# A vision tower on one core: the first pair of image groups worked through group by group, with images loaded first and products ahead of the data

## What is computed

```python
proj = patches(16x16) @ W.T + b                        # 36 patches of 768, EMBED 256
h    = concat([cls, proj]) + pos_embed                 # 37 tokens an image
q, k, v = split_heads(h @ Wq, h @ Wkv)                 # 16 heads of 64
sim  = q @ k.T / 8
G    = sigmoid(sim); P = min(reversed_cumsum(G), 63)
sim += interpolation of (q @ pos_emb) at P             # contextual positions
h    = layernorm(h + softmax(sim) @ v @ Wout + b_out)
# router over 8 experts, the best two of each token, and a shared expert
out  = layernorm(h + shared(h) + routed(h))
```

## Time and profile before

| what | us |
|---|---|
| runs | 784.12, 785.13, 785.18 (median 785.13) |
| the profiled execution | 790.15 |
| its span, first to last instruction | 788.4 |
| TensorE busy | 735.7 (93%) |
| DVE busy | 511.1 (65%) |
| ACT busy | 421.1 (53%) |
| POOL busy | 160.1 (20%) |
| mean granted TensorE clock | 0.971 |

### The profile page before, as it was taken

The page is one execution under the profiler, slowest core; times in us unless marked ns, Lnnn a source line. Parts: engine busy times, 40 slices in busy tenths (PEclk is TensorE's granted clock), DMA queues, the critical chain, the costliest instruction groups (busy, mean ns, idle before and its releaser), DMA issues. The chain is left out here.

```text
span 788.4 us, 14517 instructions
## 1 busy us (share of the span) xinstructions
PE 735.7 (93%) x5019; PEld 638.3 (81%) x5020; DVE 511.1 (65%) x1063; ACT 421.1 (53%) x780; POOL 160.1 (20%) x200
## 2 busy tenths in 40 slices
PE   5988999999999999999999979986999999999972
PEld 5867697979798897979797957775888999999862
DVE  0059898989798898989898988962442222222383
ACT  2365847565756758475656556321112555555264
POOL 2000000000000000000000000027532577776232
PEclk9999999999999999999999999988799999999997
DMA  8930001010102010010000033002001222221351
GB/s 294 315 117 17 19 24 45 23 45 23 45 0 65 3 41 27 23 34 23 12 23 12 6 119 113 23 15 25 1 2 31 66 78 83 87 83 55 141 172 71
DMA packets 28304, 47.36 MB, mean 60 GB/s; under 512 B 4794, under 2 KB 19108, under 8 KB 28275
## 3 DMA queue, kind: packets, MB, share of 16 engines
q1 hardware_dynamic: 22802, 37.24, 15.1%
q0 software_dynamic: 5472, 9.76, 4.0%
HBM read 35.57 MB, written 13.24 MB: 62 GB/s over the span
## 5 line engine op out<-in xcount | busy, mean ns | idle before, releaser
L584 POOL TENSOR_TENSOR rs<-ve,neg_half 111x2 f32<-111x2 f32 x11 | 12.5, 1133 | 472.6 <-DVE ve L1509 472.6
L758 PE MATMUL ps_X<-wkv_sb,hT 128*111 128x512 f32 (+1 forms) x176 | 85.7, 619 | 8.0 <-ACT v_sb L1150 7.5
L1034 PE MATMUL ps_S<-attnT,v_sb 128*128 128x128 f32 x704 | 85.9, 275 | 0.1
L1428 DVE COPY_PREDICATED table<-bit,table 111x112 f32<-111x112 int16 (+6 forms) x110 | 76.3, 694 | 11.4 <-DVE table L1428 0.2
L1034 PEld LDWEIGHTS ps_S<-attnT,v_sb 128*128 128x128 f32 x704 | 82.1, 192 | 0.3 <-issue 0.3
L1101 ACT COPY simS<-ps_S 32x666 f32<-32x666 f32 (+3 forms) x105 | 74.1, 705 | 13.4 <-DVE table L1485 10.5
L1758 DVE COPY attnT<-ps_S 128x256 f32<-128x256 f32 x44 | 18.7, 425 | 89.7 <-PE ps_S L1048 89.6
L758 PEld LDWEIGHTS ps_X<-wkv_sb,hT 128*111 128x111 f32 (+1 forms) x176 | 27.9, 174 | 50.7 <-issue 30.2
L699 PE MATMUL ps_S<-hT,wq_sb 128*128 128x222 f32 (+1 forms) x352 | 66.2, 345 | 0.0
L699 PEld LDWEIGHTS ps_S<-hT,wq_sb 128*128 128x128 f32 x352 | 63.5, 189 | 0.1
L794 PE MATMUL ps_X<-oT,wout_sb 128*128 128x222 f32 x320 | 61.9, 350 | 0.0
(11 more groups left out here) (212 smaller groups left out, 1383.5 us busy)
## 6 DMA issues: line engine op xcount, KB each, us to landing
down_sb<-in_x_dram SPq DMA_DIRECT2D x10, 648.0 KB
gu_sb<-y_d SPq DMA_DIRECT2D x8, 512.0 KB, 8.2
h_d<-hT SPq DMA_DIRECT2D x11, 222.0 KB, 2.7
kept<-h_d SPq DMA_DIRECT2D x11, 222.0 KB, 2.6
h_d<-h SPq DMA_DIRECT2D x10, 222.0 KB
wkv_sb<-in_L_attn_Wkv_dram SPq DMA_DIRECT2D x2, 1024.0 KB, 9.8
gu_sb<-in_L_ffn_gate_w_dram SPq DMA_DIRECT2D x2, 1024.0 KB, 11.2
gu_sb<-in_L_ffn_up_w_dram SPq DMA_DIRECT2D x2, 1024.0 KB, 12.3
```

The costliest lines, as they stand in the source:

```text
L758: mm = nc.tensor.matmul(X[:r, 1 - s], hT[:, k].rearrange("p b t -> p (b t)")[:, a * ROWS:a * ROWS + r], wkv_sb[:, k, INNER + 512 * s:INNER ...
L1034: mm = nc.tensor.matmul(S[:, i, j * FF + f * P:j * FF + f * P + P], held[:, i, k, j, f * P:f * P + P], xgT[:, i, k], start=(k == 0), stop= ...
L1428: A.did(V.copy_predicated(near[:, :, :, 0:SL - d], by_side(bit[:, n], r)[:, :, :, 0:SL - d], near[:, :, :, d:SL]))
```

## The change

- The images of pair 0 are loaded first. The token weights follow in three pieces of 256 columns, with a semaphore each. The six small loads are issued from ACT's queue.
- Half of pair 0's images is regrouped on POOL and half on DVE.
- TensorE starts with four products of the ones with the zeroed `gate` (`warm_up`), whose result is overwritten. Then it turns the patches of pair 0, and turns and multiplies the token weights piece by piece (`turn_tok`, `embed_part`). DVE, not ACT, copies the turned weights, and the two halves of an embedding (here and in pair 1) lie in two banks, and are added as each is done.
- Pair 0 has its own program, `first_pair`: keys and queries of group 0 alone (`by_group`, 111 columns), its score and values, then keys, part of the values, patches of pair 1, queries and the score of group 1. Then `embed(1)`, `keys(1)` and also `queries(1)`, before the weights of group 0 are turned. `pair(1)` is written out without its queries, and the loops of TensorE and ACT start at 2.
- DVE copies the first position table after ACT's copies of the scores, and adds `embed(1)` behind all seven parts of group 0's `cope`, not behind the fourth.

The diff, cut to its core:

```diff
+        def embedded(p, m):
+
+            if isinstance(p, int) and p < 2:
+                return X[:, m, :NPAT]
+            return X[:, 0, m * NPAT:(m + 1) * NPAT]
+
+        def of_group(bank):
+
+            return bank[:, :2 * ROWS].rearrange("p (f r) -> p f r", f=2)
+
+        KA_BANKS = [X[:, 0], S[:, 4], S[:, 5], X[:, 1]]
+        QA_BANKS = [S[:, 0], S[:, 3], S[:, 1], S[:, 2]]
+        KB_BANKS = [S[:, 0], S[:, 1], S[:, 2], S[:, 3]]
+        QB_BANKS = [S[:, 1], S[:, 2], S[:, 3], S[:, 4]]
...
+                    sp.wait_ge(xp_other, 1)
                 sp.dma_start(x_sb[:rows, :], x_rows[bass.ds(p * XR, rows), :]).then_inc(x_in, 16)
...
-            sp.dma_start(w_nat[:, :, :], tok_w.rearrange("(t p) d -> p t d", p=P)).then_inc(w_tok, 16)
             load_x(0, XR)
-            sp.dma_start(pe_nat[:TOK, :], pos_embed[0]).then_inc(w_small, 16)
...
-            for h in range(2):
-                sp.dma_start(cope_nat[DH * h:DH * h + DH, :], cope_emb).then_inc(w_small, 16)
+            for s in range(3):
+                cols = slice(2 * s * P, 2 * s * P + 2 * P)
+                sp.dma_start(w_nat[:, :, cols], tok_w.rearrange("(t p) d -> p t d", p=P)[:, :, cols]).then_inc(w_tok[s], 16)
...
-            regroup(0)
+            pool.wait_ge(x_in, 16)
+            nc.gpsimd.tensor_copy(xp_sb[:, :NPH // 2, :].rearrange("p r (i w) -> p r i w", w=PATCH),
+                                  x_halves[:, :NPH // 2]).then_inc(xp_ready, 1)
...
+                for j, bank in enumerate(second_banks if next_first(p) else patch_banks):
+                    if next_first(p) and j == 2:
+                        pe.wait_ge(k_sb, 1)
...
+            def by_group(bank, w, s, a):
+
+                for i in range(2):
+                    c = (2 * s + i) * P
+                    for k in range(KE):
+                        mm = nc.tensor.matmul(bank[:, i * ROWS:(i + 1) * ROWS], w[:, k, c:c + P],
+                                              hT[:, k, a * TPG:(a + 1) * TPG], start=(k == 0), stop=(k == KE - 1))
+                return mm
...
+                if first(p) and a == 0:
+                    pe.wait_ge(ka_sb, 4)
+                elif first(p):
+                    pe.wait_ge(k_sb, 4)
+                    pe.wait_ge(q_sb, 4)
+                    pe.wait_ge(xt_sb, 6)
+                elif a == 0:
                     pe.wait_ge(k_sb, p * 4 + 4)
                 for f in range(FT):
-                    if a == 0 and f % 3 == 0:
+                    if first(p):
+                        if a == 0 and f % 3 == 0:
+                            pe.wait_ge(qa_sb, 2 + f // 3)
+                    elif a == 0 and f % 3 == 0:
                         pe.wait_ge(q_sb, p * 4 + 2 + f // 3)
...
+            def first_pair():
+
+                pe.wait_ge(hT_ready, KE)
+                pe.wait_ge(w_k, 16)
+                for s in range(4):
+                    by_group(KA_BANKS[s], wkv_sb, s, 0).then_inc(ka_done, 1)
+                pe.wait_ge(w_q, 16)
+                for s in range(4):
+                    by_group(QA_BANKS[s], wq_sb, s, 0).then_inc(qa_done, 1)
+                pe.wait_ge(tables, N_TABLES)
+                score(0, 0)
+                for s in range(2):
+                    values(0, 0, s)
+                pe.wait_ge(sim_sb, 2)
+                pe.wait_ge(table_sb, 1)
+                for s in range(4):
+                    by_group(KB_BANKS[s], wkv_sb, s, 1).then_inc(k_done, 1)
+                values(0, 1, 0)
+                patches(1)
+                for s in range(4):
+                    if s < 3:
+                        pe.wait_ge(k_sb, s + 2)
+                    else:
+                        pe.wait_ge(xt_sb, 4)
+                    by_group(QB_BANKS[s], wq_sb, s, 1).then_inc(q_done, 1)
+                values(0, 1, 1)
+                score(0, 1)
+                pe.wait_ge(v_ready, 4)
+                pe.wait_ge(w_o, 16)
+                embed(1)
+                keys(1)
+                queries(1, True)
+                pe.wait_ge(q_sb, 4 + 2)
+                turn_weights(0, True)
+                pe.wait_ge(q_sb, 4 + 4)
+                outputs(0, 0)
+                patches(2)
+
             def pair(p, ahead, ahead2):
 
-                queries(p, ahead)
+                if next_first(p):
+                    pe.wait_ge(xt_sb, p * 3 + 6)
+                else:
+                    queries(p, ahead)
                 score(p, 0)
                 for s in range(2):
                     values(p, 0, s)
                 values(p, 1, 0)
-                if not first(p):
-                    turn_weights(p * 2 - 1, True)
+                turn_weights(p * 2 - 1, True)
                 values(p, 1, 1)
...
+            def warm_up(n):
+
+                for _ in range(n):
+                    nc.tensor.matmul(S[:, 2], ones[:, :], gate[:].rearrange("p h t -> p (h t)")[:, :512],
+                                     start=True, stop=True)
...
+            pe.wait_ge(consts, 5)
+            pe.wait_ge(zeroed, 1)
+            warm_up(4)
+            pe.wait_ge(consts, N_CONSTS)
+            pe.wait_ge(xp_other, 1)
+            patches(0)
+            turn_tok(0)
+            turn_tok(1)
+            pe.wait_ge(xt_sb, 3)
+            embed_part(0)
+            turn_tok(2)
+            embed_part(1)
...
-            pe.wait_ge(setup_sb, 1)
-            patches(0)
-            pe.wait_ge(setup_sb, 3)
-            embed(0)
-            pe.wait_ge(tables, N_TABLES)
-            pe.wait_ge(zeroed, 1)
-            keys(0)
-            patches(1)
-            pe.wait_ge(w_o, 16)
-            pair(0, True, True)
-            with pe.Fori(1, G2 - 2) as p:
+            embed_part(2)
+            first_pair()
+            pair(1, True, True)
+            with pe.Fori(2, G2 - 2) as p:
                 pair(p, True, True)
...
-                    if a == 0:
+                    if a == 0 and not first(p):
                         act.wait_ge(table_sb, g + 1)
...
+            def first_pair():
+
+                for s in range(4):
+                    act.wait_ge(ka_done, s + 1)
+                    nc.scalar.copy(kT[:, 2 * s:2 * s + 2, 0, :ROWS], of_group(KA_BANKS[s])).then_inc(ka_sb, 1)
+                for s in range(4):
+                    act.wait_ge(qa_done, s + 1)
+                    nc.scalar.copy(qT[:, 2 * s:2 * s + 2, :ROWS], of_group(QA_BANKS[s])).then_inc(qa_sb, 1)
+                for step in range(2):
+                    score(0, 0, step)
+                gates(0, 0)
+                for s in range(2):
+                    values(0, 0, s)
+                for s in range(4):
+                    act.wait_ge(k_done, s + 1)
+                    nc.scalar.copy(kT[:, 2 * s:2 * s + 2, 1, :ROWS], of_group(KB_BANKS[s])).then_inc(k_sb, 1)
+                distance(0)
+                values(0, 1, 0)
+                patches(1)
+                for s in range(4):
+                    act.wait_ge(q_done, s + 1)
+                    nc.scalar.copy(qT[:, 2 * s:2 * s + 2, ROWS:], of_group(QB_BANKS[s])).then_inc(q_sb, 1)
+                regroup(2)
+                values(0, 1, 1)
+                for step in range(2):
+                    score(0, 1, step)
+                tables_out(0, 1)
+                gates(0, 1)
+                softmax_exp(0)
+                for s in range(4):
+                    keys(1, s)
+                for s in range(4):
+                    queries(1, s)
+                weights(0)
+                distance(1)
+                outputs(0, 0)
+                patches(2)
+
             def pair(p, ahead, ahead2):
-                before = not first(p)
-                for s in range(2):
-                    queries(p, s)
+                if not next_first(p):
+                    for s in range(2):
...
-            act.wait_ge(setup_t, 3)
-            for s in range(3):
-                nc.scalar.copy(tokT[:, 2 * s:2 * s + 2], S[:, (2, 4, 5)[s]].rearrange("p (j e) -> p j e", j=2)
-                               ).then_inc(setup_sb, 1)
+            act.dma_start(pe_nat[:TOK, :], pos_embed[0]).then_inc(w_small, 16)
+            act.dma_start(pe_nat[TOK:TOK + 1, :], tok_b.rearrange("(a e) -> a e", a=1)).then_inc(w_small, 16)
...
+            for h in range(2):
+                act.dma_start(cope_nat[DH * h:DH * h + DH, :], cope_emb).then_inc(w_cope, 16)
...
-            for s in range(4):
-                keys(0, s)
-            patches(1)
             act.wait_ge(tables, N_TABLES)
-            pair(0, True, True)
-            with act.Fori(1, G2 - 2) as p:
+            first_pair()
+            pair(1, True, True)
+            with act.Fori(2, G2 - 2) as p:
...
             def embed(p):
-                dve.wait_ge(emb_done, p + 1)
                 if not first(p):
                     dve.wait_ge(h_saved, p * 16)
                 for m in range(KE):
-                    src = X[:, 0, m * NPAT:(m + 1) * NPAT].rearrange("p (c b r) -> p c b r", c=NPH, b=2 * TPG)
```

(18 more changed lines are left out.)

110 lines of the change are left out of this document (61 added, 49 removed).

## The result

| what | before | after |
|---|---|---|
| median of 5 runs each, side by side | 785.18 (784.12 to 787.36) | 779.70 (778.12 to 780.83) |
| ratio | | 0.992 (95%: 0.9899 to 0.9941) |
| profiled execution, its span | 790.15, 788.4 | 779.73, 778.0 |
| mean granted clock | 0.971 | 0.977 |
| first keys start | 22.74 | 17.26 |

The kernel is 5.5 us faster by the medians. The forecast was 776.4 (773.5 to 781.0): right in direction, inside the range, 3.3 us too low. The mark came at 77.56 against 77.1 forecast. Both kernels were run again in a second session: 785.35 (29 runs) against 776.75 (4 runs), ratio 0.9892 (0.9867 to 0.9918), which is 8.6 us. The two intervals overlap, so the runs alone don't show that the gains differ.

What follows compares the result with a forecast made beforehand. TensorE was taken to bound the kernel, busy 735.7 of 788.4 us. The 8.7 us gained early take the profiled execution from 790.15 to 781.5; less 5 us from profile to median gives 776.4 us (773.5 to 781.0).

Steps and rivals of the forecast that it cites:

- mark: Point where TensorE starts turning the second group's weights; forecast at 77.1 us, not 85.76.
- walk: TensorE's steps summed in order of time, from the start to the turning of the second group's weights: 8.7 us gained.
- given back at the loop: Rival: DVE's addition for the second pair waits for the first pair's hT save, 4 us lost, 780.4; chance 0.05.
- late save: Save of the first pair's hT, behind the expert weights in SP's queue; landing at 50 us would lose 4 us.
- 111-column product: Keys or queries of one group on TensorE: 3.2 us taken, half of the 222-column product; 3.6 by the 128-column form.
- two waits that were charged: TensorE idle before the second pair's score, for patches (1.5 us), and before the third product of values (1.5, previously 0.79).
- The parts: Gain by cause: 5.8 us head, 4.7 wait and half clock at 63 us, 1.0 shrinking waits, less 2.2: 9.3.
- last test: Whole forecast wrong if the second group's weights turn at 77 us and the end does not follow by 8.7.
- Low clock: Rival: TensorE's clock stays low through the setup, gain only 4.8 to 6.2 us, 779.6; chance 0.15.
- No new waits: Rival: ACT keeps up, so the added waits for patches and values don't arise; 10.9 us gained, 774.2; chance 0.12.
- No change: Rival: DVE or the queues, not TensorE, set the loop; 785 us; chance 0.05.
- slower: Rival: the shift puts later waits where the clock falls more often, 21 us more at half clock; 787; chance 0.05.

Runs made afterwards that it cites:

- small_on_sp: Changed kernel with its six small loads issued from SP, last of the first loads, not from ACT; 809.23 us, one run on a slower chip (kernel before: 816.18).
- head_only: Changed kernel with the new head, but the first pair and queries(1) ordered as before; 782.11 us, ratio 0.9968 to the kernel before.
- before_again: The kernel before, unchanged, run and profiled once more; median 786.27 us, ratio 1.0, profiled execution 786.43.
- one_warm: Changed kernel with one warm product in place of four; 781.06 us, ratio 0.9945 to the kernel before.

## Why the prediction was right, and where not

**The walk held at its two ends, and not in all its steps.** Forecast and measured start: patches 8.6, 8.38; keys 16.9, 17.26; first score 23.3, 24.59; second group's keys 30.2, 31.73; second score 41.6, 43.58; keys(1) 49.0, 51.22; second pair's score 67.7, 69.15; mark 77.1, 77.56. The prediction called a step wrong where it is off by more than a microsecond: by that, the five from the first score to the second pair's score failed, and the keys and the mark held. From the keys to the mark it has 60.2 us, and 60.30 came. That closeness is partly luck: the products took longer than forecast, and the waits behind them were shorter. At 399.84 and 391.65 the 8.2 us are still whole, so "given back at the loop" fell. The start of it, the late save, did too: DVE's additions for pair 1 waited for TensorE, not for the store.

```profile
48.43 0.55 DVE L1545 TENSOR_TENSOR hT<-ps_X,posb 128x216 f32<-128x216 f32 x1 [2.07 <-PE ps_X L719]
```

**Terms mis-sized.**
- The 111-column product: 3.2 forecast, 3.6 measured from its start to the next product's (3.74 to 3.79 to its own last end), four times over: 1.7 us lost. With 0.4 from the head this makes nearly all of the walk's lag of 2.2 at keys(1).
- The two waits that were charged were smaller: for patT 1.05 against 1.5, for values 0.69 against 1.5. 1.3 us came back in that way. The forecast had 3.8 us from ACT's last copy of turned weights to its last copy of patches, and they took 3.3. It also let DVE wait 3.2 us for both halves of the distance; DVE waited 2.35, for `qpos` alone. The wait for the table was larger, 1.23 against 1.0.
- Images landed at 7.27, not by 5.6. Of these 1.7 us, small_on_sp takes away 0.8; the other 0.9 no run explains. From 3 to 5 us the DMA engines move 298 and 268 GB/s with the images first, 296 and 268 in small_on_sp, where the small loads stand behind them in the same queue, and 356 and 396 in the kernel before, with the token weights first. So the forecast carried the rate of one load over to another. The warm products, ready at 7.6 and not 8.6, then hid nearly all of it: 0.75 us idle. Two errors met here.
- The parts: 5.8 from the head, and 5.5 to 6.0 came at the keys with both halves (22.74 or 23.30 to 17.26), 4.4 to 5.0 with head_only. The pair's own, 4.7 and 1.0 less 2.2, is 3.5 in the sum by parts and 2.8 in the walk; 2.7 was measured from the keys to the mark (63.02 to 60.30).

**The step that was off** was the last: "The median of the runs is 785.13, 5 us under the profiled one; I take the same difference off it". Against the profiled executions I forecast 781.5 and 779.73 came, 1.8 us better. Those 10.4 us are 8.2 at the mark, 1.3 between mark and router stretch, 0.8 in the stretch and 0.1 behind it. But after's profiled execution is at its median (779.73 and 779.70), not 5 us above. By the prediction's last test, the end was to follow by the same 8.7 us; the medians moved by 5.5 in one session and by 8.6 in the next. The profiles offer a reading. The two kinds of router stretch differ by 5 us. Before's profiled execution had the long one, while its median is where before_again's short one lies (786.43); after's had the long one as well, and by their clock most of its runs in that session had it too. In the next session the profile with the short stretch took 776.04 and the median was 776.75. That this is so near the forecast's 776.4 depends on the kind of stretch that most of the runs had, and so on chance. The clock of the other runs bears this reading out in the kernel after and not in the kernel before, and with 4 and 5 runs noise is not shut out.

**The rivals.** "Low clock" was real, but only with one warm product (one_warm). "No new waits": the waits came. "No change" and "slower" fell. The low clock of the earlier trace rows, on which "slower" rested, lies in the router stretch, whose length differs by up to 5 us between profiles of both kernels.

## What to carry to other kernels

When a change works early in a long program, choose a mark a little behind it and compare times there. It repeated here to 0.6 us in the same kernel, and the time from one mark to another to a tenth, when the end moved by about 4 us with no edit. Before adding the profile's offset to the median to a forecast, find the place in the program where the runs differ, since the changed kernel may fall on its other side. And products on zeros that fill a wait at the start can pay: here they were worth 2.5 us, what the work behind them lost at half clock without them.
